# Wide attention: who splits the weights of the later groups, and where in the unit loop

## The chip, the cores and the metric

The kernel runs on one core of a Trainium2 chip. The metric is device time in microseconds, the median of repeated runs. Five engines work side by side and wait for each other through semaphores: TensorE (PE, its weight loads are shown as PEld), VectorE (DVE), ScalarE (ACT), GpSimd (POOL) and SyncE (SP), which here issues the DMAs. The instructions of one engine run in the order in which they were written.

## The reference, cut to what matters

The program is a chain of eight stages over one residual stream of 2 x 512 tokens of width 256. The third stage is a wide attention with 16 heads of width 128:

```python
q = (x @ Wq + bq).reshape(b, h, t, dh)
k = (x @ Wk + bk).reshape(b, t, h, dh).transpose(0, 2, 3, 1)
v = (x @ Wv + bv).reshape(b, t, h, dh).transpose(0, 2, 1, 3)
logits = jnp.einsum('bhtd,bhds->bhts', q, k) * scale
weights = jax.nn.softmax(logits + mask, axis=-1)
out = jnp.einsum('bhts,bhsd->bhtd', weights, v)
return out.transpose(0, 2, 1, 3).reshape(b, t, h * dh) @ Wo + bo
```

## The kernel before

The stage is the function wide_stage. The 16 heads are worked on in 4 groups of 4 heads, and each group for both batches: a "unit" is one pair of group i and batch b, so there are 8 units of 4 heads. The function `units` writes the loop: three turns of a hardware loop (i = 0, 1, 2) with two units each, (i, 0) and (i, 1), and the two units of the last group behind it. Every engine writes its own copy of it. In the trace the turn with i = 0 runs from about 759 to 861 us of the span, the next two from there to about 960 and 1060 us.

Precision: a product of two f32 matrices is made of three matmuls in fp32r, from a high and a low part of each operand (lines 78, 79 and 80 of the helper `product`). So each weight tile has to be split before use: high = rounded copy of raw, low = raw - high. For each group there are three weight tiles of 128 x 1024, raw in `w_raw`: part 0 for k, part 1 for v, part 2 for the output projection. `w_raw`, `w_hi` and `w_lo` hold one group only. SP loads them in the function `load(i)`, in this order: it waits until all k tiles of the group before are evacuated (`k_done`), loads the k bias and the k weights; it waits until all v tiles of the group before are evacuated (`v_done`), loads the v bias (line 831), the v weights and the output weights (line 834). Each load also waits until the split that last read its part of `w_raw` is done (`w_split`).

Before the change POOL splits all parts of groups 1 to 3: line 853 writes the high part (an addition of zero), line 856 the low part, each time after a wait that the old parts were last read (`k_ready`, `v_ready` or `out_done`) and a wait that the raw weights have landed (`w_loaded`). Behind each group's three splits stands `move_q` (line 863), a copy of 128 x 2048 q values for batch 1, which needs the scores of the group before to be issued and the 8 q tiles of its own group to be evacuated, and which PE needs only in the last head of unit (i, 0).

Filling: while PE works through the heads of one unit, it also computes ("fills") the k, q and v tiles of the next unit, through one PSUM bank. In unit (i, 0) these are 4 k tiles (heads 0 and 1) and 4 v tiles (heads 2 and 3) of (i, 1), with the weights of group i. In unit (i, 1) they are 8 q tiles (heads 0 and 1), 4 k tiles (head 2) and 4 v tiles (head 3) of (i + 1, 0), with the weights of group i + 1. So the k weights of group i + 1 are first needed in the third head of unit (i, 1), the v weights in its fourth head, the output weights in the first head of unit (i + 1, 0). q and v tiles are evacuated by DVE (lines 1092 and 1101), k tiles by ACT.

One head in PE's order: transposes of the head's probabilities, rows 0 and 1, then row 2 (`turn` 0 and 1, line 945); scores of the next head, first bank (line 932, with the mask of line 934); transposes of row 3 (`turn` 2), which wait until ACT has copied the first transposes out of PSUM (`probs_t_done`, because they use the same bank); more scores; a fill; `attend` (line 951), which waits for all of ACT's copies of the transposes (line 1033); a fill; the last scores; `project_out`. ACT's order in a head: copies for turn 0 and 1 (line 1033), exponentials of the next head's rows 0 and 1 (line 1025, behind DVE's row maxima of line 1106), copy for turn 2 (line 1033), more exponentials, high part of the head's output (line 1059), the last exponentials. DVE's order: row maxima (line 1106) and normalisation (reciprocal line 1113, multiplication line 1116) of the next head, evacuation of a fill, low part of the output (line 1142), the last row's maximum and normalisation, evacuations; at the end of a unit it adds the unit's two result banks to the residual stream (`add_to_stream`, line 1122, behind `out_done`).

Of the kernel before, what the change touches and what calls it, by code (L numbers as in the profile page):

```python
# [5 lines left out]
ALU = mybir.AluOpType  # L6
ACT = mybir.ActivationFunctionType
# [7 lines left out]
P = 128  # L15
B, S, D = 2, 512, 256
# [3 lines left out]
DC = D // P  # L20
# [25 lines left out]
def f32(ap):  # L46

    return ap.bitcast(F32)
# [52 lines left out]
class Norm:  # L101
# [45 lines left out]
    def low_parts(self, dve):  # L147
        for k in range(NHALF * DC):
            dve.wait_ge(self.hi_done, k + 1)
            dve.tensor_tensor(self.half_of(self.res.xl, k), self.turned_half(k), f32(self.half_of(self.res.xh, k)),  # L150
                              ALU.subtract).then_inc(self.lo_done, 1)
# [587 lines left out]
GROUP = 4  # L739
GROUPS = HEADS // GROUP  # L740
WIDE = GROUP * DH
# [5 lines left out]
def wide_stage(nc, name, res, t):  # L747
# [6 lines left out]
    with ExitStack() as ctx:  # L754
# [12 lines left out]
        w_raw = sb("w_raw", [P, 3, DC * WIDE])  # L767
        w_hi, w_lo = sb("w_hi", [P, 3, DC * WIDE], F32R), sb("w_lo", [P, 3, DC * WIDE], F32R)
# [8 lines left out]
        w_loaded = [sem(f"w_loaded{p}") for p in "kvo"]  # L777
        w_hi_done = sem("w_hi_done")
        w_split = [sem(f"w_split{p}") for p in "kvo"]
        bias_loaded, bk_loaded, bv_loaded, bq_scaled = sem("bias_loaded"), sem("bk_loaded"), sem("bv_loaded"), sem("bq_scaled")  # L780
        k_ready, v_ready, q_ready = sem("k_ready"), sem("v_ready"), sem("q_ready")
# [4 lines left out]
        o_ready, o_hi_done, o_lo_done, out_done = sem("o_ready"), sem("o_hi_done"), sem("o_lo_done"), sem("out_done")  # L786
# [10 lines left out]
        def score_bank(h, r):  # L797

            return s_bank[(3 * h + UNIT_OF_ROW[r]) % 2][:, ROW_AT[r]:ROW_AT[r] + (r + 1) * P]

        def turned_bank(h, u):
            return t_bank[(3 * h + u) % 2]

        def units(engine, unit):

            with engine.Fori(0, GROUPS - 1) as i:
                for b in range(B):
                    unit(i, b, True)
            for b in range(B):
                unit(GROUPS - 1, b, b == 0)  # L810

# [32 lines left out]
        @block.gpsimd  # L844
        def _(pool):
            norm.gpsimd(pool)

            def split(i, some):
                for p in some:
                    used = (k_ready, v_ready, out_done)[p]  # L850
                    pool.wait_ge(used, B * GROUP * i)
                    pool.wait_ge(w_loaded[p], 16 * i + 16)
                    pool.tensor_tensor(w_hi[:, p, :], w_raw[:, p, :], res.zero[:].broadcast_to([P, DC * WIDE]),
                                       ALU.add).then_inc(w_hi_done, 1)
                    pool.wait_ge(w_hi_done, 3 * i + p)
                    pool.tensor_tensor(w_lo[:, p, :], w_raw[:, p, :], f32(w_hi[:, p, :]),
                                       ALU.subtract).then_inc(w_split[p], 1)

            def move_q(i):

                pool.wait_ge(scores_ready, 3 * B * GROUP * i)
                pool.wait_ge(q_done, Q_FILLS * (i + 1))
                pool.tensor_tensor(q[:, 1, :], q_next[:], res.zero[:].broadcast_to([P, GROUP * S]),
                                   ALU.add).then_inc(q_moved, 1)

            split(0, (1, 2))
            move_q(0)
            pool.wait_ge(norm.normed, NT)
            pool.wait_ge(bias_loaded, 32)
            pool.tensor_tensor(res.x[:], res.x[:], bo[:].unsqueeze(1).broadcast_to([P, NT, D]), ALU.add).then_inc(bo_added, 1)  # L870
            with pool.Fori(1, GROUPS) as i:
                split(i, (0, 1, 2))
                move_q(i)

        @block.tensor
        def _(pe):
# [129 lines left out]
            for u in range(3):  # L1006
                scores(0, 0, 0, u)
            units(pe, unit)

        @block.scalar  # L1010
        def _(act):
            norm.scalar(act)
            act.wait_ge(w_loaded[0], 16)
            act.activation(w_hi[:, 0, :], w_raw[:, 0, :], ACT.Copy).then_inc(k_hi_done, 1)
            act.wait_ge(wq_loaded, 16 * DC)
            act.activation(wq_hi[:], wq_raw, ACT.Copy).then_inc(wq_hi_done, 1)

            def k_evacuated(U, b, f, bank):
                act.wait_ge(k_ready, GROUP * U + f + 1)
                act.activation(k[:, b, f, :], bank[:], ACT.Identity, bias=bk[:, f:f + 1]).then_inc(k_done, 1)  # L1020

            def exponentials(h, n, u):
                for r in UNIT_ROWS[u]:
                    act.wait_ge(max_done, 4 * n + max(r, 1) + 1)
                    act.activation(probs[:, h % 2, r, 0:(r + 1) * P], score_bank(h, r), ACT.Exp,  # L1025
                                   bias=neg_max[:, 4 * h + r:4 * h + r + 1],
                                   accum_out=row_sum[:, 4 * h + r:4 * h + r + 1]).then_inc(exp_done, 1)

            def turned_back(h, n, u):
                act.wait_ge(turned, 3 * n + u + 1)  # L1030
                for r in UNIT_ROWS[u]:
                    from_ = turned_bank(h, u)[:, ROW_AT[r]:ROW_AT[r] + (r + 1) * P].rearrange("p (j q) -> p j q", q=P)
                    last = act.activation(probs_t[:, 0:r + 1, r * P:(r + 1) * P], from_, ACT.Copy)  # L1033
                last.then_inc(probs_t_done, 1)

            def unit(i, b, more):
                U = B * i + b
                for h in range(GROUP):
                    n = GROUP * U + h
                    after, follows = ((h + 1) % GROUP, n + 1), more or h + 1 < GROUP  # L1040
                    fills = fills_of_step(i, b, h, more)

                    def next_fills(fills):
                        for i1, b1, kind, f in fills:
                            if kind == "k":
                                if f == 0:
                                    act.wait_ge(bk_loaded, 16 * i1 + 16)
                                k_evacuated(B * i1 + b1, b1, f, fill_bank)

                    turned_back(h, n, 0)  # L1050
                    turned_back(h, n, 1)
                    if follows:
                        exponentials(*after, 0)
                    turned_back(h, n, 2)
                    if follows:
                        exponentials(*after, 1)
                    next_fills(fills[0])
                    act.wait_ge(o_ready, n + 1)
                    act.activation(o_hi[:], o_bank[:], ACT.Copy).then_inc(o_hi_done, 1)
                    next_fills(fills[1])  # L1060
                    if follows:
                        exponentials(*after, 2)
                    next_fills(fills[2] + fills[3])

            act.wait_ge(bk_loaded, 16)
            for f in range(GROUP):
                k_evacuated(0, 0, f, ring[f])
            act.wait_ge(wq_split, 1)
            for u in range(3):
                exponentials(0, 0, u)  # L1070
            units(act, unit)

        @block.vector
        def _(dve):
# [49 lines left out]
            def unit(i, b, more):  # L1124
                U = B * i + b
                for h in range(GROUP):
                    n = GROUP * U + h
                    after, follows = ((h + 1) % GROUP, n + 1), more or h + 1 < GROUP
                    fills = fills_of_step(i, b, h, more)

                    def next_fills(fills):
                        for one in fills:
                            evacuated(*one, fill_bank)

                    if follows:
                        row_max(*after, 0)
                        row_max(*after, 1)
                        normalise(*after, 0)
                        normalise(*after, 1)
                    next_fills(fills[0])  # L1140
                    dve.wait_ge(o_hi_done, n + 1)
                    dve.tensor_tensor(o_lo[:], o_bank[:], f32(o_hi[:]), ALU.subtract).then_inc(o_lo_done, 1)
                    next_fills(fills[1])
                    if follows:
                        row_max(*after, 2)
                        normalise(*after, 2)
                    next_fills(fills[2] + fills[3])
                add_to_stream(U, b)

            for g, (kind, f) in enumerate(FIRST_FILLS):  # L1150
                evacuated(0, 0, kind, f, ring[g % 4])
            for u in range(3):
# [1 line left out]
            for u in range(3):  # L1154
                normalise(0, 0, u)
            dve.wait_ge(bo_added, 1)
            units(dve, unit)


Q_HEADS, KV_HEADS, HD = 16, 4, 16  # L1160
# [1632 lines left out]
```

## Time and profile before

| | us |
|---|---|
| median of 3 runs | 1934.93 |
| lowest and highest run | 1932.46 and 1941.78 |
| the profiled execution, its time | 1930.95 |
| the profiled execution, its span | 1929.2 |
| PE busy in the span | 1555.1 (81%) |
| PEld busy | 1199.5 (62%) |
| DVE busy | 998.2 (52%) |
| ACT busy | 845.8 (44%) |
| POOL busy | 400.8 (21%) |

All rows come from one profiled execution, so a sum of durations is to be set against its own time. "Busy" leaves out register, branch and semaphore instructions, and the ends of matmuls are modelled. The shares are means over eight stages with different limits; what the change is worth is to be read in the stage of the wide attention, about 712 to 1141 us of the span.

### The profile page before, as it was taken

The numbers are of one execution on the slowest core, as the hardware profiler recorded it, in microseconds if no ns is written. First come the engines' busy times: TensorE is split into PE (matmuls) and PEld (weight loads), VectorE is DVE, ScalarE is ACT, GpSimd is POOL, SyncE is SP. The second block draws the span as 40 slices with busy tenths as digits, with TensorE's granted clock in tenths as the row PEclk, the third lists the DMA queues.
The fourth block names the chain that finished last, engine by engine and source line by source line (L and its number), as shares of the span: only waits on it lengthen the run. The fifth ranks groups of instructions, "written<-read, shape, count | busy, mean of one in ns | idle before, by whom it ended". The sixth has DMA issues, their size and how long they took to land. (4 is left out here: it accounts for less than half of the span.)

```text
span 1929.2 us, 29951 instructions
## 1 busy us (share of the span) xinstructions
PE 1555.1 (81%) x10280; PEld 1199.5 (62%) x10280; DVE 998.2 (52%) x2341; ACT 845.8 (44%) x2214; POOL 400.8 (21%) x340
## 2 busy tenths in 40 slices
PE   4977968868849958999999879957788797689695
PEld 3766757757747746676767657745666575533473
DVE  4535634635646155555565556156766641557632
ACT  4544544534423423334343433415666433378332
POOL 1201201212011622111111101622000035110053
PEclk9987988979969978999999999978999899799797
DMA  2101101101033230101010022220000233100423
GB/s 89 45 1 50 34 2 49 34 12 39 23 101 133 91 126 17 39 1 38 0 37 2 1 95 112 93 81 6 6 5 0 80 121 107 56 1 1 151 76 116
DMA packets 43588, 100.03 MB, mean 52 GB/s; under 512 B 7504, under 2 KB 22224, under 8 KB 43216
## 3 DMA queue, kind: packets, MB, share of 16 engines
q1 hardware_dynamic: 33488, 70.11, 10.7%
q0 software_dynamic: 9984, 28.32, 4.5%
q8 instruction: 78, 1.28, 0.3%
q14 instruction: 38, 0.31, 0.1%
HBM read 80.06 MB, written 18.35 MB: 51 GB/s over the span
## 5 line engine op out<-in xcount | busy, mean ns | idle before, releaser
L2137 POOL TENSOR_TENSOR s_w_hi<-s_w_raw,zero 128x1024 fp32r<-128x1024 f32 x20 | 37.8, 1891 | 436.3 <-PE s_work L80 344.4
L426 PE MATMUL s_bank<-s_expert_w,s_xe 128*128 x368 | 124.9, 462 | 2.1 <-ACT s_xe L542 1.4
L718 DVE TENSOR_TENSOR s_h_e<-s_bank,s_silu_e 128x176 f32<-128x176 f32 x92 | 31.4, 341 | 181.2 <-ACT s_silu_e L548 181.1
L300 POOL DMA_INDIRECT s_xg<-normed_rows,s_from_row x92 | 91.0, 989 | 124.7 <-DVE s_from_row L672 97.9
L307 POOL DMA_INDIRECT expert_rows<-s_y,s_to_row x92 | 91.1, 990 | 97.5 <-ACT s_y L560 80.4
L1025 ACT ACTIVATE s_scratch<-s_bank,s_neg_max 128x128 f32<-128x128 f32 (+3 forms) x128 | 67.2, 528 | 88.9 <-DVE s_neg_max L1106 88.9
L173 PE MATMUL s_bank<-ident,s_ln_xn 128*128 128x128 f32 x112 | 25.7, 424 | 98.8 <-DVE s_ln_xn L134 98.8
L78 PE MATMUL s_bank<-xn_t_hi,s_w_hi 128*128 128x512 f32 x224 | 97.1, 433 | 5.8 <-DVE s_w_lo L1079 4.8
L450 PE MATMUL s_bank<-s_expert_w,s_he 88*128 x368 | 95.7, 382 | 4.9 <-ACT s_he L554 4.9
L1106 DVE TENSOR_REDUCE s_neg_max<-s_bank 128x1 f32<-128x128 f32 (+3 forms) x128 | 59.7, 487 | 75.7 <-PE s_bank L934 75.6
L951 PE MATMUL s_bank<-s_probs_t,s_v 128*128 128x512 f32 (+3 forms) x256 | 76.2, 441 | 20.5 <-ACT s_probs_t L1033 20.5
L932 PE MATMUL s_bank<-s_k,s_q 128*128 128x128 f32 (+3 forms) x256 | 89.9, 447 | 3.0 <-ACT s_scratch L1025 2.2
L79 PE MATMUL s_bank<-xn_t_lo,s_w_hi 128*128 128x512 f32 x224 | 91.5, 409 | 0.0
L80 PE MATMUL s_bank<-xn_t_hi,s_w_lo 128*128 128x512 f32 x224 | 91.2, 407 | 0.0
L78 PE MATMUL s_work<-xn_t_hi,s_w_hi 128*128 128x512 f32 x128 | 59.5, 464 | 35.7 <-ACT s_positive L2375 33.2
L450 PEld LDWEIGHTS s_bank<-s_expert_w,s_he 88*128 88x128 f32 x368 | 69.1, 190 | 29.7 <-issue 6.9
L1384 ACT ACTIVATE s_probs<-s_bank,s_neg_max 128x128 f32<-128x128 f32 (+3 forms) x128 | 67.3, 529 | 46.2 <-DVE s_neg_max L1455 45.9
L1825 ACT ACTIVATE s_exps<-s_bank,s_rms 128x512 f32<-128x512 f32 x128 | 76.6, 695 | 20.4 <-PE s_bank L1711 20.4
L173 PEld LDWEIGHTS s_bank<-ident,s_ln_xn 128*128 128x128 f32 x112 | 22.4, 224 | 101.1 <-DVE s_ln_xn L134 100.7
L1313 PE MATMUL s_bank<-ident,s_probs 128*128 128x128 f32 x320 | 57.6, 297 | 29.3 <-DVE s_q_lo L1441 14.5
L951 PEld LDWEIGHTS s_bank<-s_probs_t,s_v 128*128 128x128 f32 x256 | 46.5, 189 | 55.0 <-ACT s_probs_t L1033 25.7
L1455 DVE TENSOR_REDUCE s_neg_max<-s_bank 128x1 f32<-128x128 f32 (+3 forms) x128 | 59.6, 486 | 35.7 <-PE s_bank L1302 35.3
(332 smaller groups left out, 4657.1 us busy)
## 6 DMA issues: line engine op xcount, KB each, us to landing
s_expert_w<-in_experts SPq DMA_DIRECT2D x32, 608.0 KB, 12.8
s_w_raw<-in_wa_o SPq DMA_DIRECT2D x16, 512.0 KB, 3.7
s_yg<-expert_rows SPq DMA_DIRECT2D x32, 256.0 KB, 4.4
s_raw<-in_shared SPq DMA_DIRECT2D x16, 384.0 KB, 5.4
normed_rows<-s_ln_xn POOLq DMA_DIRECT2D x8, 512.0 KB, 9.6
s_w_raw<-in_wa_k SPq DMA_DIRECT2D x4, 512.0 KB, 4.6
s_w_raw<-in_wa_q SPq DMA_DIRECT2D x4, 512.0 KB, 3.5
s_w_raw<-in_wa_v SPq DMA_DIRECT2D x4, 512.0 KB, 3.5
```

The source lines that it names most:

```text
L78: pe.matmul(out, sh, mh, start=first, stop=False, skip_group_check=True)
L79: pe.matmul(out, sh, ml, start=False, stop=False, skip_group_check=True)
L80: return pe.matmul(out, sl, mh, start=False, stop=last, skip_group_check=True)
L300: pool.indirect_dma_start(out=xg[:, i % XG_RING, :], out_offset=None, in_=x_rows[:, :], in_offset=bass.IndirectOffsetOnAxis(ap=from_row[:, ...
L307: pool.indirect_dma_start(out=y_rows[:, :], out_offset=bass.IndirectOffsetOnAxis(ap=to_row[:, i:i + 1].bitcast(U32), axis=0), in_=y[:, i % ...
L426: last = pe.matmul(u_bank[i % 2][:, 0:2 * INTER], xe[:, i % 2, x], expert_of(P, i, w), start=c == 0, stop=c == DC - 1, skip_group_check=True)
L450: last = pe.matmul(y_bank[i % 2][:, 0:D], he[0:IHALF, i % 2, h], expert_of(IHALF, i, w), start=c == 0, stop=c == 1, skip_group_check=True)
L932: pe.matmul(to, q[:, b, h * S + r * P:h * S + (r + 1) * P], k[:, b, h, 0:(r + 1) * P], start=r == UNIT_ROWS[u][0], stop=False, skip_group_ ...
L951: last = pe.matmul(o_bank[:, j * P:S], v[:, b, j, h * DH:(h + 1) * DH], probs_t[:, j, j * P:S], start=j == 0, stop=j == TB - 1, skip_group ...
L1025: act.activation(probs[:, h % 2, r, 0:(r + 1) * P], score_bank(h, r), ACT.Exp, bias=neg_max[:, 4 * h + r:4 * h + r + 1], accum_out=row_sum ...
L1384: act.activation(probs[:, g % 2, r, 0:(r + 1) * P], s_bank[u][:, ROW_AT[r]:ROW_AT[r] + (r + 1) * P], ACT.Exp, bias=neg_max[:, 4 * g + r:4 ...
L1825: act.activation(exps[:, s % 2, g, :], s_bank[g][:], ACT.Exp, scale=rms[:, b, 1, j:j + 1]).then_inc(exp_done, 1)
```

## The change

From group 1 on the split of the weights is no longer POOL's. ACT writes the high parts (a copy on the activation engine, `high_parts`) and DVE the low parts (`low_parts`). Both do it at fixed points in their unit loops: the parts 0 and 1 (k and v) of group i + 1 between unit (i, 0) and unit (i, 1), and part 2 (output) of group i + 1 behind unit (i, 1). Each part has the same waits as before in front of its high part, now on ACT. The low part waits for its high part. Group 0 is split as before (ACT and DVE for k, POOL for v and output), and POOL keeps `move_q`. SP's loads and all of PE's instructions are unchanged.

```diff
-        def units(engine, unit):
+        def units(engine, unit, between=None):
 
             with engine.Fori(0, GROUPS - 1) as i:
-                for b in range(B):
-                    unit(i, b, True)
+                unit(i, 0, True)
+                if between is not None:
+                    between(i + 1, (0, 1))
+                unit(i, 1, True)
+                if between is not None:
+                    between(i + 1, (2,))
             for b in range(B):
                 unit(GROUPS - 1, b, b == 0)
...
-            def split(i, some):
-                for p in some:
-                    used = (k_ready, v_ready, out_done)[p]
-                    pool.wait_ge(used, B * GROUP * i)
-                    pool.wait_ge(w_loaded[p], 16 * i + 16)
-                    pool.tensor_tensor(w_hi[:, p, :], w_raw[:, p, :], res.zero[:].broadcast_to([P, DC * WIDE]),
-                                       ALU.add).then_inc(w_hi_done, 1)
-                    pool.wait_ge(w_hi_done, 3 * i + p)
-                    pool.tensor_tensor(w_lo[:, p, :], w_raw[:, p, :], f32(w_hi[:, p, :]),
-                                       ALU.subtract).then_inc(w_split[p], 1)
+            def first_split(p):
+                pool.wait_ge(w_loaded[p], 16)
+                pool.tensor_tensor(w_hi[:, p, :], w_raw[:, p, :], res.zero[:].broadcast_to([P, DC * WIDE]),
+                                   ALU.add).then_inc(w_hi_done, 1)
+                pool.wait_ge(w_hi_done, p)
+                pool.tensor_tensor(w_lo[:, p, :], w_raw[:, p, :], f32(w_hi[:, p, :]),
+                                   ALU.subtract).then_inc(w_split[p], 1)
...
-            split(0, (1, 2))
+            first_split(1)
+            first_split(2)
             move_q(0)
...
             with pool.Fori(1, GROUPS) as i:
-                split(i, (0, 1, 2))
                 move_q(i)
...
+            def high_parts(i, some):
+
+                for p in some:
+                    act.wait_ge((k_ready, v_ready, out_done)[p], B * GROUP * i)
+                    act.wait_ge(w_loaded[p], 16 * i + 16)
+                    act.activation(w_hi[:, p, :], w_raw[:, p, :], ACT.Copy).then_inc(w_hi_done, 1)
...
-            units(act, unit)
+            units(act, unit, high_parts)
...
+            def low_parts(i, some):
+
+                for p in some:
+                    dve.wait_ge(w_hi_done, 3 * i + p)
+                    dve.tensor_tensor(w_lo[:, p, :], w_raw[:, p, :], f32(w_hi[:, p, :]), ALU.subtract).then_inc(w_split[p], 1)
...
-            units(dve, unit)
+            units(dve, unit, low_parts)
```

## Rows read from the trace of the kernel before

**Rows 1.** Busy time by stretch, one whole unit (columns: PE, PEld, DVE, ACT, POOL, clock, DMA, GB/s):
```profile
885.00:942.00 57.00, 53.45 (x317) 41.70 (x316) 36.31 (x84) 20.31 (x61) 8.54 (x4) 1.00 0.09 31
```
**Rows 2.** Waits of PE, 750 to 1140 us (waiter <- releaser: total us, times, longest):
```profile
PE s_bank L951 <- ACT s_probs_t L1033: 20.5, 20, 1.4
PE s_bank L78 <- DVE s_v L1101: 3.2, 3, 1.1
```
**Rows 3.** Timeline of SP (start us, duration), load of group 1's v weights:
```profile
808.02 0.38 SPq L834 DMA_DIRECT2D s_w_raw<-in_wb_v  x1
```
**Rows 4.** Timeline of POOL: high parts of k and v, move_q (idle before <- releaser):
```profile
787.48 1.89 POOL L853 TENSOR_TENSOR s_w_hi<-s_w_raw,zero 128x1024 fp32r<-128x1024 f32 x1 [32.40 <-DMA s_w_raw<-in_wb_k]
...
813.43 1.89 POOL L853 TENSOR_TENSOR s_w_hi<-s_w_raw,zero 128x1024 fp32r<-128x1024 f32 x1 [21.60 <-DMA s_w_raw<-in_wb_v]
...
863.40 3.60 POOL L863 TENSOR_TENSOR s_q<-s_q_next,zero 128x2048 f32<-128x2048 f32 x1
...
913.65 1.89 POOL L853 TENSOR_TENSOR s_w_hi<-s_w_raw,zero 128x1024 fp32r<-128x1024 f32 x1 [22.13 <-DMA s_w_raw<-in_wb_v]
...
1013.09 1.89 POOL L853 TENSOR_TENSOR s_w_hi<-s_w_raw,zero 128x1024 fp32r<-128x1024 f32 x1 [21.87 <-DMA s_w_raw<-in_wb_v]
```
**Rows 5.** Timeline of ACT around the seam between units (0, 0) and (0, 1):
```profile
806.06 0.19 ACT L1025 ACTIVATION_READ_ACCUMULATOR s_scratch<-s_bank,s_neg_max 128x1 f32 x1
808.01 0.94 ACT L1033 ACTIVATE s_probs_t<-s_bank 128x128 f32<-128x128 f32 x3 [1.76 <-PE s_bank L945]
809.82 0.37 ACT L1025 ACTIVATE s_scratch<-s_bank,s_neg_max 128x128 f32<-128x128 f32 x1 [0.87 <-DVE s_neg_max L1106]
```
**Rows 6.** Timeline of PE: third transposes behind three seams, and two waits:
```profile
793.30 0.50 PE L78 MATMUL s_bank<-s_w_hi,xn_t_hi 128*128 128x512 f32 x1 [1.07 <-DVE s_v L1101]
...
808.96 0.61 PE L945 MATMUL s_bank<-ident,s_scratch 128*128 128x128 f32 x4
...
864.60 2.42 PE L951 MATMUL s_bank<-s_probs_t,s_v 128*128 128x512 f32 x8 [1.32 <-ACT s_probs_t L1033]
...
908.64 0.61 PE L945 MATMUL s_bank<-ident,s_scratch 128*128 128x128 f32 x4
...
1008.35 0.61 PE L945 MATMUL s_bank<-ident,s_scratch 128*128 128x128 f32 x4
```
**Rows 7.** Groups by form, whole program (count, busy us, mean ns, idle before):
```profile
L2383 ACT ACTIVATE s_w_hi<-s_w_raw 128x1024 fp32r<-128x1024 f32 x8 | 8.4, 1059 | 24.0 <-PE s_memory L80 24.0
L2457 DVE TENSOR_TENSOR s_w_lo<-s_w_raw,s_w_hi 128x1024 fp32r<-128x1024 f32 x8 | 9.7, 1219 | 17.0 <-ACT s_w_hi L2383 17.0
```
**Rows 8.** Timeline of DVE: normalisations beside POOL's work and without it, and row maxima:
```profile
787.61 1.92 DVE L1116 TENSOR_SCALAR s_scratch<-s_scratch,s_row_sum 128x256 f32<-128x256 f32 x1
789.63 2.42 DVE L1116 TENSOR_SCALAR s_scratch<-s_scratch,s_row_sum 128x384 f32<-128x384 f32 x1
...
809.16 0.62 DVE L1106 TENSOR_REDUCE s_neg_max<-s_bank 128x1 f32<-128x128 f32 x2 [0.19 <-PE s_bank L934]
...
811.36 0.35 DVE L1116 TENSOR_SCALAR s_scratch<-s_scratch,s_row_sum 128x256 f32<-128x256 f32 x1
...
812.01 0.42 DVE L1116 TENSOR_SCALAR s_scratch<-s_scratch,s_row_sum 128x384 f32<-128x384 f32 x1
...
862.50 0.61 DVE L1106 TENSOR_REDUCE s_neg_max<-s_bank 128x1 f32<-128x128 f32 x2
...
863.98 3.09 DVE L1116 TENSOR_SCALAR s_scratch<-s_scratch,s_row_sum 128x128 f32<-128x128 f32 x1
```
**Rows 9.** Busy time by stretch, other stages (columns as in group 1): a gap, and restarts:
```profile
1797.50:1802.80 5.30, 0.00 (x0) 0.00 (x0) 5.17 (x4) 0.00 (x0) 0.00 (x0) 0.83 0.00 0
1802.80:1806.00 3.20, 2.93 (x12) 2.63 (x12) 0.18 (x1) 0.00 (x0) 0.00 (x0) 0.50 0.00 0
292.20:299.00 6.80, 6.79 (x44) 6.80 (x45) 3.38 (x4) 2.66 (x3) 1.89 (x1) 0.74 0.01 2
1535.70:1545.00 9.30, 8.49 (x36) 6.99 (x36) 5.98 (x11) 4.32 (x7) 1.71 (x3) 0.68 1.02 370
```

## The prediction

> **What bounds the kernel now.** I read the page first. PE is busy 81% of the span, but that is a mean over eight stages, and the change lives in one of them. So I asked for the busy time by stretch inside the wide attention. In one whole unit PE is busy 53.45 of 57 us at a granted clock of 1.00, DVE 36.31, ACT 20.31 and POOL 8.54 [rows 1]. PE sets the pace of this stage. What stops PE costs time one for one, and work on DVE or ACT is free as long as PE finds its inputs ready.
>
> Next came the list of PE's waits in the stage. No wait of PE on POOL is in it. The longest in total is attend waiting for ACT's copies of the transposes, 20.5 us in 20 waits of at most 1.4 us. A small one is a fill waiting for the evacuation of the v tile before it, 3.2 us in 3 waits [rows 2]. So POOL's splits are nowhere late: taking them earlier can bring nothing by itself. What they cost is indirect, and the timelines of POOL and DVE show it. While POOL splits the k weights (from 787.48, [rows 4]) two normalisations on DVE take 1.92 and 2.42 us, where the same two forms take 0.35 and 0.42 beside an idle engine or other work [rows 8]. Beside `move_q` (863.40, 3.60 us, [rows 4]) a normalisation of the smallest form takes 3.09 us [rows 8]. The last view was the timeline of SP, ACT, DVE and PE at the two seams at which the change puts its work.
>
> **What is removed.** Nine high and nine low parts on POOL, with their place beside DVE. The k split holds DVE for (1.92 - 0.35) + (2.42 - 0.42) = 3.6 us in each of three groups. Most of it falls into slack. What reaches PE is the wait of 1.07 us at 793.30, one of the three waits for the v evacuation, at most 1.1 each [rows 6, 2]. I credit -1.07 x 3 = -3.2 us. Beside the v split (813.43) the normalisation at 812.01 keeps its 0.42 us [rows 4, 8], so I credit nothing there.
>
> **What moves without being written.** `move_q` no longer stands behind the split of the output weights. It then starts when the last scores of the unit's fourth head are issued, some 20 us earlier, in the third head of unit (i, 1). It would hold one normalisation there for up to 3.6 us. In that head the fills are k tiles, which ACT evacuates, and DVE has nothing due before the next head. I cost it at nothing. If that cover is missing, it is what it is now in another place: between 0 and the 3.09 - 0.35 = 2.7 us by which DVE is now held at 863.98 [rows 8], per group. SP's order does not change. The waits on `w_split` that its loads have are passed earlier than the `k_done` and `v_done` waits in front of them.
>
> **What is added between (i, 0) and (i, 1): a wait for a transfer.** This is the term that decides. SP can issue the v weights only when the last v tile of unit (i, 0) is evacuated, that is at the very end of the unit: 808.02 [rows 3]. They land when POOL, which waits for them, starts: 813.43, a good 5 us later [rows 4]. For POOL that wait was harmless. ACT has finished its part of the unit at 806.25 (the last accumulator read, [rows 5]). It now makes the k high part (1.06 us by the group of the same form, [rows 7]) until about 807.3 and then stands at the wait for the v weights until 813.43. Behind it on ACT is everything for the next unit, first the copies of the transposes that start at 808.01 now [rows 5]. PE has no choice: its third transposes, at 808.96 now [rows 6], use the bank of the first and wait for the first of these copies.
>
> So ACT makes the v high part at 813.43, 1.06 us, and the first of its three copies (a third of 0.94, 0.31 us, [rows 5]), and with 0.1 us for the signals PE goes on at about 813.43 + 1.47 = 814.90 instead of 808.96: 5.9 us. The same for the second group, 913.65 + 1.47 - 908.64 = 6.5, and the third, 1013.09 + 1.47 - 1008.35 = 6.2 [rows 4, 6]. Sum 18.6 us. DVE runs into the same wall: it makes the k low part (1.22 us, [rows 7]) and then waits for ACT's v high part until 814.5, its v low part ends at 815.7, and its row maxima start there instead of at 809.16, 6.5 us late [rows 8]. ACT's exponentials (809.82 now) follow these maxima [rows 5]. That is the same delay as PE's within 0.6 us, on a parallel path, so it is not added. PE works at 94% here, so hardly any of it is made up later.
>
> **The clock behind the gap.** In the stage of this change the granted clock is 1.00, that is 2.4 GHz [rows 1]. In a later stage PE stands still for 5.30 us and the clock falls inside that gap (mean 0.83), and the 3.20 us behind it run at 0.50, 1.2 GHz [rows 9]. A gap of about 6 us should do the same here. What that costs I take from two restarts: 6.80 us at a mean of 0.74, which is 1.8 us of lost clock, and 9.30 us at 0.68, which is 3.0 us [rows 9]. I take 2.0 per gap, nearer to the restart in which PE was busy throughout, as it will be here: 6.0 us. The bounds are 0 (the clock stays up) and 9.0. The Trainium skill, TensorE: Matmul & The Clock Gate, section HAM oscillation, speaks against this change: a DMA wait between bursts of matmuls throttles PE, and each next burst starts cold. By that rule the sum keeps this term; a reader who doubts it reads the sum as 19.1 instead of 25.1 us.
>
> **What is added behind (i, 1): a delay on DVE.** ACT's high part of the output weights waits for the last `project_out`, which is followed by a fill, and fits into time in which ACT waits anyway. DVE has no such gap: its row maxima at 862.50 start without any idle time before them, right behind the addition to the stream, and attend at 864.60 already waits 1.32 us at the end of the chain maxima, exponentials, copy [rows 8, 6]. The low part stands in front of the maxima, 1.22 us [rows 7], and all of it reaches attend: 1.22 x 3 = 3.7 us. The bounds are 0 and, if the two-operand subtraction were held as long as POOL's own low part, some 2.4 us per group; POOL is idle there now, so I take the first form.
>
> **Sum.** 18.6 + 6.0 + 3.7 - 3.2 = 25.1 us. The profiled execution took 1930.95 us, so this gives 1956.0. That execution lies 4.0 us under the median of the runs, 1934.93, and the forecast for a median is 1960.0 us, 1.3% slower.
>
> **Rivals.**
>
> *The clock stays up.* The same stalls, no loss of clock: 18.6 + 3.7 - 3.2 = 19.1 us, 1954. The gap would be short enough to pass. For it: the fall in the 5.30 us gap came late in it [rows 9]. Chance 0.10.
>
> *The relief pays for the stall (the other side).* POOL and DVE hold each other up, for 3.6 us beside the k split and 2.7 us beside `move_q` in each group [rows 8]. If all of that now reached PE, the relief would be 6.3 x 3 = 18.9 instead of 3.2 us, and the sum 28.3 - 18.9 = 9.4 us, 1944; with the clock up it is 3.4 us, 1938, which no measurement would tell from before. It decides at 28.3 / 3 = 9.4 us of relief per group for a gain. Against it: PE's wait behind the hold is 1.07 us [rows 6]. The Trainium skill, GPSIMD Engine Reference, Specifications, gives the rule behind this rival: POOL shares its memory interfaces with VectorE and contends with instructions that use two ports or two inputs in SBUF. The trace agrees that there is a hold, 2.42 for 0.42 us; it is silent on who is late afterwards. Chance 0.04 for a time within 0.5%, 0.02 for a faster one.
>
> *The v weights have landed when ACT gets there.* Then ACT's two high parts end at 806.25 + 2.12 = 808.4, hardly late, and DVE's two low parts push the maxima by 2.4 us. Sum (2.4 + 1.2 - 1.1) x 3 = 7.5 us, 1942, within 0.5%. For it: only that loads of the other parts are early. Against it: the issue at 808.02 is behind a DVE evacuation at the end of the unit, and the landing is 5.4 us behind it; POOL waited over 21 us for each of the three [rows 3, 4]. Chance 0.04.
>
> *Late things pile up.* The restart at half clock and DVE's 6.5 us late maxima add up instead of lying side by side, or `move_q` now lands where DVE has no slack (2.7 per group): 25.1 + 3.0 + 8 = 36 us, 1971. Chance 0.08.
>
> **How the numbers follow.** The forecast has 0.72. About 0.5% (10 us) is what a measurement of this kernel can tell from no change. Slower by more than that: 0.72 + 0.10 + 0.08 = 0.90, within it 0.04 + 0.04 = 0.08, faster 0.02. The range: below, the clock stays up and the delay on DVE is absorbed, 19.1 - 3.7 = 15.4 us, 1950; above, the clock costs 9.0 instead of 6.0, and the two late paths add their 0.6 us and a few us of spread between runs (1932.46 to 1941.78): 1969.
>
> **What the profile after would show.** Right: three idle gaps of PE of 5.5 to 7 us in the wide stage, at the third transposes (line 945), released by ACT's copies; ACT's v high part waiting 5 to 6 us for the DMA of the v weights, three times; a clock below 1.00 in the few us behind each gap; attend in the first head of unit (i + 1, 0) waiting about 2.5 instead of 1.32 us; no normalisation on DVE of 1.9 or 2.4 us at the end of k loads; `move_q` some 20 us before the end of unit (i, 1), with one long normalisation beside it and no wait of PE. Wrong would be: v weights that are already there when ACT arrives, a PE that goes on in the gap, or a stage that is shorter although the gaps are there, which would mean that the relief was under-priced.

## The result: 1.45% slower, and the profile after

| | before | after |
|---|---|---|
| median, us | 1936.43 (6 runs) | 1964.44 (6 runs) |
| lowest to highest, us | 1931.48 to 1941.78 | 1957.75 to 1971.98 |
| ratio, 95% interval | | 1.0145 [1.0112, 1.0178] |
| profiled execution, its time | 1930.95 | 1971.98 |
| its span | 1929.2 | 1970.2 |
| wide stage in it | 431.1 | 461.5 |

The profiled execution of after is the slowest of its six runs. Of the 41 us by which its span is longer, 8.7 us lie ahead of the wide stage and some 2 us behind it, in code that the change doesn't touch. So in all that follows I measure the stage, not the program: from SP's first load in it (the k bias) to SP's first load of the next stage. The place between unit (i, 0) and unit (i, 1) I call the first seam, the place behind unit (i, 1) the second seam. In the timeline of SP of the changed kernel (start us, duration):

```profile
720.99 0.35 SPq L831 DMA_DIRECT2D s_bk<-in_bb_k  x1
...
791.70 0.34 SPq L831 DMA_DIRECT2D s_bk<-in_bb_k  x1
...
1182.51 0.34 SPq L272 DMA_DIRECT2D s_gate_raw<-in_gate  x1
```

1182.51 - 720.99 = 461.5 us, 30.4 more than the 431.1 of before. The beginning of the stage, up to SP's load for group 1 (its ramp), takes 70.3 to 71.1 us in the kernels whose edits don't touch it, and up to 73.0 in two whose edits do. The part behind that load is the sharper measure for the loop, and I call it the loop part: 1182.51 - 791.70 = 390.8 us, against 360.0 before (783.37 to 1143.38 in the same view). The difference is 30.8 us. Each kernel has one profile. How well such a stretch repeats can be seen where no edit reaches: from attend in the second head of unit (3, 0) to the first load of the next stage it took 67.92 to 67.98 us in all ten profiles, those from the other chip (below) included.

The timeline of ACT at the seam behind unit (0, 0) (start us, duration, in brackets idle before and releaser), to be set beside [rows 5]:

```profile
813.23 0.19 ACT L1026 ACTIVATION_READ_ACCUMULATOR s_scratch<-s_bank,s_neg_max 128x1 f32 x1
813.32 1.05 ACT L1071 ACTIVATE s_w_hi<-s_w_raw 128x1024 fp32r<-128x1024 f32 x1
820.74 1.06 ACT L1071 ACTIVATE s_w_hi<-s_w_raw 128x1024 fp32r<-128x1024 f32 x1 [6.37 <-DMA s_w_raw<-in_wb_v]
821.70 0.91 ACT L1034 ACTIVATE s_probs_t<-s_bank 128x128 f32<-128x128 f32 x3
```

The k part runs at once, then ACT waits 6.37 us for the v weights, and the copies for PE start only behind both. The timeline of DVE shows the same wall, and the row maxima that follow it:

```profile
816.05 1.22 DVE L1162 TENSOR_TENSOR s_w_lo<-s_w_raw,s_w_hi 128x1024 fp32r<-128x1024 f32 x1
821.83 1.23 DVE L1162 TENSOR_TENSOR s_w_lo<-s_w_raw,s_w_hi 128x1024 fp32r<-128x1024 f32 x1 [4.56 <-ACT s_w_hi L1071]
822.97 0.62 DVE L1114 TENSOR_REDUCE s_neg_max<-s_bank 128x1 f32<-128x128 f32 x2
```

In the timeline of PE there are three gaps of 6.07, 6.39 and 6.27 us at the third transposes (the long gaps), and attend in the first head of unit (1, 0) waits 2.46 us where it waited 1.32 us [rows 6]. This wait and the two like it, 2.46 and 2.54 us, are the short gaps:

```profile
822.36 0.90 PE L946 MATMUL s_bank<-ident,s_scratch 128*128 128x128 f32 x3 [6.07 <-ACT s_probs_t L1034]
...
882.02 0.70 PE L952 MATMUL s_bank<-s_probs_t,s_v 128*128 128x512 f32 x1 [2.46 <-ACT s_probs_t L1034]
...
933.08 0.68 PE L946 MATMUL s_bank<-ident,s_scratch 128*128 128x128 f32 x2 [6.39 <-ACT s_probs_t L1034]
...
1042.96 0.47 PE L946 MATMUL s_bank<-ident,s_scratch 128*128 128x128 f32 x1 [6.27 <-ACT s_probs_t L1034]
```

The busy time by stretch (columns: PE, PEld, DVE, ACT, POOL, clock, DMA, GB/s), first the stretches in which PE goes on behind the three long gaps (the restarts), then those behind the three short ones:

```profile
822.40:832.40 10.00, 10.00 (x42) 7.42 (x42) 5.51 (x15) 2.89 (x9) 0.00 (x0) 0.70 0.00 0
933.10:943.10 10.00, 9.81 (x45) 7.43 (x46) 6.23 (x16) 2.91 (x9) 0.00 (x0) 0.78 0.00 0
1043.00:1053.00 10.00, 9.81 (x48) 7.43 (x49) 6.33 (x16) 3.04 (x10) 0.00 (x0) 0.81 0.00 0
...
882.00:888.00 6.00, 5.98 (x16) 3.97 (x17) 1.34 (x4) 1.60 (x4) 0.00 (x0) 0.72 0.00 0
992.00:998.00 6.00, 5.98 (x16) 3.62 (x17) 1.34 (x4) 1.56 (x4) 0.00 (x0) 0.72 0.00 0
1101.80:1107.80 6.00, 6.00 (x17) 3.42 (x17) 1.28 (x3) 1.60 (x4) 0.00 (x0) 0.75 0.00 0
```

The clock, 1.00 throughout this part of the stage before, is down behind all six gaps. Lost clock is length times one minus the mean: 3.0 + 2.2 + 1.9 = 7.1 us behind the long gaps, 1.7 + 1.7 + 1.5 = 4.9 us behind the short ones. With the gaps of PE (18.7), the longer waits of attend ((2.46 - 1.32) and two like it, 3.4) and the lost wait for the v evacuation (-3.2, it is gone from the list of waits), that makes 30.9 us. The loop part is 30.8 longer. The busy time of the whole loop part gives the same split without choosing stretches: the same 1853 matmuls are busy 343.04 us instead of 331.20, at a mean clock of 0.96 instead of 1.00, which is 11.8 us, and PE is idle 19.0 us more.

### The profile page after: what moved, and what is told of

Same layout as the page of the kernel before. It is cut to its first block and busy times, and to the rows that moved or that the text cites. A ratio compares the mean times of both kernels' runs of the same rounds, so it can differ in the third digit from the quotient of the medians.

```text
span 1970.2 us, 29946 instructions
## 1 busy us (share of the span) xinstructions
PE 1575.9 (80%) x10280; PEld 1214.0 (62%) x10280; DVE 996.0 (51%) x2350; ACT 856.0 (43%) x2223; POOL 363.2 (18%) x322
## 5 line engine op out<-in xcount | busy, mean ns | idle before, releaser
L952 PE MATMUL s_bank<-s_probs_t,s_v 128*128 128x512 f32 (+3 forms) x256 | 81.7, 465 | 23.3 <-ACT s_probs_t L1034 23.3
```

The costliest lines, as they stand in the source:

```text
L952: last = pe.matmul(o_bank[:, j * P:S], v[:, b, j, h * DH:(h + 1) * DH], probs_t[:, j, j * P:S], start=j == 0, stop=j == TB - 1, skip_group ...
```

## The experiments

The kernels with one part, and the one with v loaded early, ran on another chip, on which the kernel before took 1972.14 us (12 runs, 1966.42 to 1979.54). The last four ran on a chip on which it took 1934.84 us (17 runs, 1931.69 to 1945.19). Times are compared only on the same chip, stages across all.

| kernel | wide stage | loop part | loop part against before |
|---|---|---|---|
| before | 431.1 | 360.0 | |
| changed | 461.5 | 390.8 | +30.8 |
| v part only | 456.8 | 386.1 | +26.1 |
| k part only | 428.8 | 358.3 | -1.7 |
| output part only | 437.1 | 366.7 | +6.7 |
| v loaded early | 443.1 | 370.1 | +10.1 |
| first seam kept busy | 452.4 | 381.3 | +21.3 |
| both seams kept busy | 452.4 | 379.8 | +19.8 |
| before, `move_q` early | 431.2 | 360.5 | +0.4 |
| parts in slack | 427.1 | 356.3 | -3.8 |

**One part at a time.** Each of three kernels hands one of the three parts to ACT and DVE, at the place that the change has for it, and leaves the other two to POOL. For v (the others are alike):

```diff
-                    between(i + 1, (0, 1))
+                    between(i + 1, (1,))
...
-                    between(i + 1, (2,))
+                    between(i + 1, ())
...
             with pool.Fori(1, GROUPS) as i:
+                for at, p in enumerate((0, 2)):
+                    pool.wait_ge((k_ready, v_ready, out_done)[p], B * GROUP * i)
+                    pool.wait_ge(w_loaded[p], 16 * i + 16)
...
                 move_q(i)
```

> Only the v weights of groups 1 to 3 are split by ACT and DVE between the two units; POOL keeps k and the output weights. The length of the wide stage is read from SP's first load in it to SP's first load of the next stage: 431.1 us before the change, 461.5 after it. Theory (the wait for the landing of the v weights): this part alone has nearly the whole cost, three idle gaps of PE of about 6.2 us and some 7 us of lost clock, stage 455 to 458. Rival (the cost is the work of ACT and DVE itself, the same for each of the nine parts): a third of the cost, 441.

> Only the k weights of groups 1 to 3 are split by ACT and DVE between the two units, POOL keeps the rest. They have landed long before. Theory: PE's wait of 1.07 us for a v evacuation goes in each group (-3.3), the low part makes DVE's row maxima about 1 us late and attend waits 0.7 to 1.0 us (+2 to +3), stage 430 to 431. Rival (the work itself costs): 441.

> Only the output weights of groups 1 to 3 are split by ACT and DVE, behind unit (i, 1); POOL keeps k and v. Theory: attend in the first head of the next unit waits 2.5 instead of 1.3 us (+3.5 in all), and the clock falls in this short gap as it does after the change, another 3 to 5 us: stage 438 to 440, with three falls of the clock at these seams only. If the clock needs the 6 us gap at the other seam to fall here too, the stage is 434.6. Rival (the work itself costs): 441, but without a longer wait of attend.

Measured: stages of 456.8, 428.8 and 437.1 us. The rival, a cost of the work itself, would have given 441 for each and is out: three times six instructions of the same length cost +26.1, -1.7 and +6.7 us, by where they wait. The three add up to 31.1, the whole change is 30.8. The time of the single run of the v kernel was 1995.85 us, above all runs of before on that chip; those of the k and output kernels were 1967.39 and 1971.31, inside its spread.

In the list of PE's waits of the v kernel (waiter <- releaser: total us, times, longest) the three long gaps stand alone, and the waits for the v evacuation are still there, because POOL still splits k:

```profile
PE s_bank L955 <- ACT s_probs_t L1043: 18.6, 3, 6.4
PE s_bank L961 <- ACT s_probs_t L1043: 18.2, 17, 1.4
PE s_bank L78 <- DVE s_v L1118: 3.0, 3, 1.0
```

The k kernel has the reverse: no wait on the evacuation of v in its list, nothing above 1.4 us in the loop. Its gain is a little larger than the expected 0 to 1 us. In the output kernel the three short gaps are 2.46, 2.46 and 2.55 us, but the clock fell behind only two of them, where three falls were expected; so its stage is 0.9 us under the expected 438 to 440. By stretch, behind each:

```profile
876.70:882.70 6.00, 5.92 (x23) 4.00 (x24) 2.09 (x5) 2.30 (x6) 0.00 (x0) 1.00 0.00 0
977.70:983.70 6.00, 5.96 (x16) 3.80 (x17) 1.36 (x4) 1.59 (x4) 0.00 (x0) 0.72 0.00 0
1080.20:1086.20 6.00, 5.97 (x16) 3.83 (x17) 1.27 (x3) 1.45 (x4) 0.00 (x0) 0.72 0.00 0
```

That prices a fall. From SP's load for one group to that for the next, the turn without it took 895.21 - 794.40 = 100.81 us, the one with it 997.84 - 895.21 = 102.63. Before had 99.66 and 99.80 for these two turns. So the low part in front of the maxima is worth 100.81 - 99.66, a good 1.1 us, and the fall the rest of 102.63 - 99.80, another 1.7.

**The landing by itself.** The changed kernel with SP's loads in another order:

```diff
-                sp.wait_ge(v_done, B * TB * i)
-                sp.dma_start(bv[:], t["bb_v"][bass.ds(i, 1), :].rearrange("a n -> (a n)").partition_broadcast(P)).then_inc(bv_loaded, 16)
                 for p in (1, 2):
                     sp.wait_ge(w_split[p], i)
...
+                sp.wait_ge(v_done, B * TB * i)
+                sp.dma_start(bv[:], t["bb_v"][bass.ds(i, 1), :].rearrange("a n -> (a n)").partition_broadcast(P)).then_inc(bv_loaded, 16)
```

> The changed kernel, but SP issues the loads of the v and output weights ahead of its wait for the v evacuations instead of behind it; only the bias of v stays behind it. Theory (landing): the v weights are there when ACT comes, the 6 us gaps go. What stays is DVE's 2.4 us for two low parts in front of the row maxima, an attend that waits 2 to 3 us, and perhaps a clock that falls there for one spell: stage 440 to 447, time 15 to 22 us below the changed kernel. Rival (the work itself costs): no change, 461.

Measured: stage 443.1, loop part +10.1 instead of +30.8; 1982.66 us against 1972.14 for before on that chip, ratio 1.0051 [1.0031, 1.0070]. The changed kernel itself was not timed on that chip, so the 15 to 22 us can be judged by the stage alone: 18.4 us less. SP issues the v weights 22 us before the seam (795.56), ACT makes both high parts without a break, and DVE both low parts:

```profile
816.19 1.99 ACT L1071 ACTIVATE s_w_hi<-s_w_raw 128x1024 fp32r<-128x1024 f32 x2
818.09 0.92 ACT L1034 ACTIVATE s_probs_t<-s_bank 128x128 f32<-128x128 f32 x3
```
```profile
818.92 2.35 DVE L1162 TENSOR_TENSOR s_w_lo<-s_w_raw,s_w_hi 128x1024 fp32r<-128x1024 f32 x2
821.19 1.08 DVE L1114 TENSOR_REDUCE s_neg_max<-s_bank 128x1 f32<-128x128 f32 x3
```

What is left at this seam is a wait of attend of 1.50 to 1.52 us, less than the expected 2 to 3, and the clock stays up behind it. So it was the landing that made the gap, not the work. The second seam is as in the changed kernel: attend waits 2.46, 2.46 and 2.55 us, and the six microseconds behind it run at 0.72, 0.72 and 0.74. The first of them by stretch:

```profile
877.60:883.60 6.00, 5.99 (x16) 4.00 (x17) 1.33 (x4) 1.62 (x4) 0.00 (x0) 0.72 0.00 0
```

**The clock by itself.** The changed kernel with matmuls that compute nothing of use, in the time in which PE has to wait. Their result goes into a bank that attend overwrites:

```diff
+            def keep_busy(n):
+
+                for _ in range(n):
+                    pe.matmul(o_bank[:], res.ident_bf[:], res.zeros[:], start=True, stop=True, skip_group_check=True)
...
+                    if (b, h) == (1, 0) and not isinstance(i, int):
+                        keep_busy(24)
                     turn(h, n, 2)
```

> The changed kernel with 24 extra matmuls (128x512, zeros in bf16, into the idle bank of attend, whose result is never read) in front of PE's third transposes in the first head behind the first seam, in the three loop turns: about 5.1 of the 6.2 us in which PE has to wait there anyway. Theory (the clock falls because PE is idle in the gap and costs 7.1 us in three restarts): granted clock 1.00 behind this seam, PE's wait there about 1 us, stage 461.5 - 7 = 454 to 455. Rival (the slow restart belongs to the restart itself, not to the idle time): clock and stage as before, 461.5.

> As the run with extra matmuls at the first seam, and 9 more (about 1.9 us) in front of attend in the first head of each unit (i, 0), where the changed kernel waits 2.46 us. Theory (the 2.5 us gap also drops the clock, which the forecast left out): clock 1.00 behind the second seam too, some 4 us less in three restarts, against about 1.3 us more in the first turn, where that gap is short: stage 451 to 453. Rival (that gap costs only its 1.1 us more of waiting): no gain at the second seam, 455 to 456.

Measured: 452.4 and 452.4 us of stage (single runs of 1961.28 and 1951.67 us; 8.7 us of their difference lie ahead of the stage, in code that both share). With the long gaps filled, the 10 us behind the first seam run at 1.00 in all three turns. Busy time by stretch in the kernel with only these gaps filled, the first two rows behind long gaps, the last three behind the short gaps, which it leaves as they are:

```profile
820.70:830.70 10.00, 9.79 (x61) 7.76 (x62) 7.27 (x19) 3.61 (x11) 0.00 (x0) 1.00 0.00 0
927.20:937.20 10.00, 9.76 (x61) 7.76 (x62) 7.29 (x19) 3.64 (x11) 0.00 (x0) 1.00 0.00 0
...
877.70:883.70 6.00, 5.95 (x23) 4.04 (x24) 2.06 (x5) 2.31 (x5) 0.00 (x0) 1.00 0.00 0
984.20:990.20 6.00, 5.99 (x16) 3.94 (x17) 1.33 (x4) 1.60 (x4) 0.00 (x0) 0.72 0.00 0
1092.10:1098.10 6.00, 6.00 (x23) 4.01 (x24) 1.96 (x4) 2.25 (x5) 0.00 (x0) 1.00 0.01 3
```

Nothing but PE's idle time was changed at the first seam, and the 42, 45 and 48 matmuls in the 10 us behind it became 61 each time. The matmuls added stand ahead of these stretches and are not counted in them. The stage is some 2 us under the expected 454 to 455. The gain, 9.5 us of loop part, is more than the 7.1 of these restarts, because behind the short gaps, which are as long as before, the clock fell once instead of three times: two falls fewer, some 3.4 us (the two together are 1 us more than what was gained). With the short gaps filled too it fell nowhere, and the loop part is another 1.5 us shorter, one fall. The stage is not, because its ramp was 1.5 us longer in that run: the extra matmuls also stand in the first turn, where there is hardly a gap. That the stage came out within the expected 451 to 453 is luck: the gain and the loss were both sized for three falls, and the first of the two kernels already had only one. So this second run, as I had set it up, could show the fall only in the turn that had one: 1004.30 - 896.17 = 108.1 us with it, 995.35 - 888.95 = 106.4 without; the turn ahead of these, which had no fall in either, took 106.12 and 106.15 us.

**The moved copy.** The kernel before with one edit:

```diff
-                split(i, (0, 1, 2))
-                move_q(i)
+                split(i, (0, 1))
+                move_q(i)
+                split(i, (2,))
```

> The kernel before with one edit: POOL does its copy of q in front of its split of the output weights instead of behind it, so that it starts in the third head of unit (i, 1), as in the changed kernel. Forecast's term (this move costs nothing and gains nothing): stage 431.1 within 0.5 us, a normalisation of some 2 us beside the copy at the new place and no new wait of PE. Rival (DVE's hold of 2.7 us beside this copy reaches PE at the old place or at the new one): stage 423 or 439.

Measured: stage 431.2 (a single run of 1941.28 us) and PE's waits as before. The timeline of POOL and of DVE at the new place:

```profile
852.17 3.60 POOL L863 TENSOR_TENSOR s_q<-s_q_next,zero 128x2048 f32<-128x2048 f32 x1 [25.56 <-PE s_bank L935]
```
```profile
853.78 2.28 DVE L1117 TENSOR_SCALAR s_scratch<-s_scratch,s_row_sum 128x512 f32<-128x512 f32 x1
857.82 0.29 DVE L1107 TENSOR_REDUCE s_neg_max<-s_bank 128x1 f32<-128x128 f32 x1 [1.76 <-PE s_bank L935]
```

The normalisation is held (2.28 us; the one at this place took 0.49 before, at 845.01), and DVE still waits 1.76 us for PE behind it. At the old place POOL now does nothing, and the smallest form takes 0.29 us there instead of the 3.09 of before. Attend behind it waits 1.32 us all the same, as before. In the timelines of DVE and PE:

```profile
872.77 0.29 DVE L1117 TENSOR_SCALAR s_scratch<-s_scratch,s_row_sum 128x128 f32<-128x128 f32 x1
...
873.39 2.42 PE L952 MATMUL s_bank<-s_probs_t,s_v 128*128 128x512 f32 x8 [1.32 <-ACT s_probs_t L1034]
```

The hold is real and costs nothing, at the old place and at the new one.

**The parts in slack.** The change's idea with other places:

```diff
+        def parts_in(i, b, h):
+
+            if (b, h) == (0, 0):
+                return [(i, 2)]
+            if isinstance(i, int):
+                return []
+            return {(0, 3): [(i + 1, 0)], (1, 1): [(i + 1, 1)]}.get((b, h), [])
...
                     next_fills(fills[0])
+                    for g, p in parts_in(i, b, h):
+                        if p == 2:
+                            act.wait_ge(acc_read, signals(2 * B * g))
+                        else:
+                            act.wait_ge((k_ready, v_ready)[p], B * GROUP * g)
+                        act.wait_ge(w_loaded[p], 16 * g + 16)
+                        act.activation(w_hi[:, p, :], w_raw[:, p, :], ACT.Copy).then_inc(high_done[p], 1)
                     act.wait_ge(o_ready, n + 1)
...
                     next_fills(fills[0])
+                    for g, p in parts_in(i, b, h):
+                        dve.wait_ge(high_done[p], g + 1 if p == 2 else g)
+                        dve.tensor_tensor(w_lo[:, p, :], w_raw[:, p, :], f32(w_hi[:, p, :]), ALU.subtract).then_inc(w_split[p], 1)
                     dve.wait_ge(o_hi_done, n + 1)
```

> Changed kernel with the parts spread out: ACT's high part stands directly in front of its wait for attend and DVE's low part directly in front of its wait for ACT's high part of the output, one part per head: k weights of group i + 1 in the last head of unit (i, 0), v weights in the second head of unit (i, 1), output weights of group i in the first head of unit (i, 0), for group 0 too. SP's order is that of the changed kernel. ACT waits about 2 us and DVE 1.9 us there anyway. Theory (only the place and the landing matter): no new wait of PE above 1.5 us, the clock stays at 1.00, the wait of 1.07 us beside the k split is gone: stage 427.5 to 429, time 2 to 4 us under the kernel before, at the edge of what can be told. Rival (nine parts cost ACT and DVE time wherever they stand): stage 440 or more.

POOL's split of the output weights of group 0 and the functions `high_parts` and `low_parts` are gone from it (not shown).

Measured: stage 427.1, loop part 3.8 us under before, and its mean clock is 1.00. Ten parts were split on ACT and ten on DVE, and in the list of PE's waits between 780 and 1140 us nothing is longer than 1.4 us:

```profile
PE s_bank L960 <- ACT s_probs_t L1042: 18.8, 18, 1.4
PE s_bank L78 <- DVE s_o_lo L1161: 3.0, 4, 1.4
PE s_bank L78 <- DVE s_q_next L1108: 1.2, 6, 0.2
```

The whole kernel took 1934.29 us against 1934.84, ratio 0.9986 [0.9965, 1.0008]. It is the fastest of all in the stage and better than the changed kernel. But in the time of the whole program its gain over the kernel before, 0.55 us where 2 to 4 were expected, cannot be told from none.

## Why the prediction was right

**The wait for the landing** was the cause, as forecast, and its size too: 18.6 us forecast, 18.7 measured in the changed kernel, 18.6 with the v part alone. That PE stops at the third transposes, and that DVE's own delay lies beside and not on top of it, can be read in the three gaps. What the early load showed is stronger than the rows: with the landing gone the rest at this seam is under 2 us. ACT's waits for the v weights were 6.37, 6.69 and 6.56 us, a little over the 5 to 6 that the prediction named as a sign; its own times, 807.3 to 813.43, already gave 6.1.

**The clock behind the long gaps**: 6.0 us forecast from two restarts of other stages, 7.1 measured. Filling the gap kept the clock at 1.00, so idle time of PE is the cause. The rule of the Trainium skill, TensorE: Matmul & The Clock Gate, section HAM oscillation, is that a DMA wait between bursts makes the next burst start cold. The trace agrees: behind the three waits for the landing, 10 us run at a mean clock of 0.70, 0.78 and 0.81.

**The delay on DVE at the second seam**: 3.7 us forecast, 3.4 measured. But the step said that "all of it reaches attend" and stopped there. I gave the clock a term only where the gap was 6 us, although the same step made attend's wait 2.5 us long. It fell there too, three times, for 4.9 us. This is the term that was missing, and it is nearly the whole difference between the forecast sum, 25.1, and the 30.8 us of the loop part. The clock as a whole cost 7.1 + 4.9 = 12.0 us, more than the 9.0 that the prediction had as its upper bound. No row of before shows a restart behind a 2.5 us gap that the argument had used, so the honest bound would have been 0 to three further falls.

**The relief**: 3.2 us forecast, and the waits on the v evacuation are gone from the changed kernel, 3.2 us. The k part alone gives -1.7, since its low part on DVE takes some of it back. The rival that all of DVE's holds would now reach PE fell with the k part alone, which gains 1.7 us and not 3.6 x 3, and with the moved copy: its 2.7 us per group are worth nothing in either place. Two readings of the prediction were off here, without effect on its sum. The 2.7 compares two forms; the held form takes 0.29 us where POOL is idle, so the hold is 2.8. And the normalisation at 812.01 ends at 812.43, a microsecond before the v split begins: it is not beside it. DVE has no normalisation at all while POOL splits v there (813.43 to 817.78), so nothing to credit is right, for another reason. The Trainium skill, GPSIMD Engine Reference, section Specifications, says that POOL shares its SBUF interfaces with VectorE and contends with instructions in a two-port mode or with two inputs in SBUF. The trace agrees that there is a hold, 2.28 us for 0.49, and does not show by which of the two; in the time of the stage it does not appear.

**The other rivals.** The v weights had not landed when ACT came; in the kernel in which they had, the loop part is 10.1 us over before, where the rival had put 7.5. Two things hide in this difference of 2.6: the clock behind the short gaps adds some 5 us, and attend waits 1.5 us at the first seam where the rival had 2.4, which takes 2.7 back. The clock did not stay up. Nothing piled up at the seams beyond the clock: with it, the gaps and waits add up to the whole difference.

**The median**: 1964.44 against 1960.0 forecast. In medians the change is 28.0 us (22 to 34 by the interval), between the forecast sum and the profiled difference of the stage. Of the 4.4 us by which the forecast is low, 1.5 are the median of before, 1936.43 with six runs and 1934.93 with the three that the forecast had. The time lies inside the range, 1950 to 1969, although the cost of the clock lies outside its bound. That is in part luck: the medians moved by less than the 30.8 us of the stage in the one profile, and the upper end had a few us for the spread between runs.

## What to carry to other kernels

Before work goes from an idle engine to a busy one, look at its waits, not at its length: on POOL a wait of over 21 us for the v weights was free, on ACT the last 6 us of it stopped everything queued behind. At a fixed point of an in-order queue a step may only wait for what is surely there by then; here an earlier load took the long gaps away, and so did places one head and more later. And each new wait of PE should be priced twice, as idle time and as the slow restart that may follow it, even when it is only 2.5 us long.

## What the hardware showed that I had not expected

- A gap of PE of only 2.45 to 2.55 us was followed by a spell at 1.2 GHz in 9 of 12 cases (3 of 3 in the changed kernel, 3 of 3 with the early load, 2 of 3 with the output part alone, 1 of 3 with the first seam filled), and each cost about 1.7 us. Behind waits of 1.5 us and less at the same seams it was not seen. In the changed kernel the fall came at different points: behind the first short gap the first microsecond still ran at 0.96 and the next three at 0.50, behind the third the first microsecond was already at 0.50. What decides between the nine and the three is open; PE's instructions around the gap are the same.
- One and the same kernel, the one before, has a median of 1972.14 us on one chip and 1934.84 on another, 1.9% apart. The kernel before was not profiled on the first, but the others show where: behind the wide stage the profiles there have 808 to 820 us, all others 786 to 793. Two executions of the same code differ by some 9 us ahead of the stage. In the stage itself, stretches without an edit agree within 0.1 us, so kernels could be told apart there by less than 1 us.
